# Graph-attention walks in steps of one tile of 128 edges instead of two, with eight tiles of each chunk scaled by ScalarE alone

## What is computed

```python
def gat_conv(x, W, a_src, a_dst, bias, src, dst, heads, out_ch, concat):
    h = (x @ W).reshape(n, heads, out_ch)
    al_s = jnp.einsum('nhc,hc->nh', h, a_src)
    al_d = jnp.einsum('nhc,hc->nh', h, a_dst)
    logits = jax.nn.leaky_relu(al_s[src] + al_d[dst], NEG_SLOPE)
    m = jax.ops.segment_max(logits, dst, num_segments=n)
    e = jnp.exp(logits - m[dst])
    denom = jax.ops.segment_sum(e, dst, num_segments=n)
    msg = h[src] * (e / denom[dst])[:, :, None]
    out = jax.ops.segment_sum(msg, dst, num_segments=n)
...
xn = _layernorm(x)
x = x + gnn(xn, edge_index, ...) + mix(xn, ...)
x = x + ffn(_layernorm(x), ...)
```

## Time and profile before

| what | us |
|---|---|
| median of 3 runs | 5648.19 (5645.58 to 5658.97) |
| the profiled execution, its own time | 5653.59 |
| its span from the first to the last instruction | 5651.8 |
| mean granted TensorE clock, as a share of full speed | 0.858 |
| POOL busy | 3660.6 |
| PE busy | 4335.7 |
| DVE busy | 3078.8 |
| ACT busy | 3010.0 |
| the walk of layer 1, first to last rescaling (L1268) | 223.7 to 2329.4 |
| the walk of layer 2, the same | 2565.1 to 4647.1 |

### The profile page before, as it was taken

How to read it: one execution, slowest core, us unless ns; L and a number is a source line. 1 busy time by engine, 2 the same in 40 slices (tenths; PEclk the granted TensorE clock), 3 DMA queues, 4 the chain that set the end, 5 groups by cost and what they waited for, 6 DMA issues and landing times. The chain is left out here.

```text
span 5651.8 us, 82730 instructions
## 1 busy us (share of the span) xinstructions
PE 4335.7 (77%) x21069; PEld 3336.5 (59%) x21069; DVE 3078.8 (54%) x8587; ACT 3010.0 (53%) x10079; POOL 3660.6 (65%) x3778
## 2 busy tenths in 40 slices
PE   7588888888888888775766667666565656899998
PEld 4466666666666666553444444444444435788887
DVE  5477777777777777654545545454454548211111
ACT  2677777777777777674545455453333334122221
POOL 0577777777777777457777777777777762344443
PEclk9789899999999998897778777787777775999999
DMA  5788878888888888435455444444556547443332
GB/s 188 236 242 242 243 234 244 241 243 241 243 243 244 240 243 238 144 119 145 138 143 143 138 144 138 143 140 140 170 159 171 159 119 238 143 129 129 127 127 74
DMA packets 427478, 1021.41 MB, mean 181 GB/s; under 512 B 115224, under 2 KB 207632, under 8 KB 426758
## 3 DMA queue, kind: packets, MB, share of 16 engines
q0 software_dynamic: 229312, 718.64, 44.4%
q1 hardware_dynamic: 197142, 296.44, 15.7%
q10 hardware_dynamic: 560, 1.05, 0.1%
HBM read 952.23 MB, written 65.48 MB: 180 GB/s over the span
## 5 line engine op out<-in xcount | busy, mean ns | idle before, releaser
L871 POOL DMA_INDIRECT walk_ring<-s_h,walk_index x3320 | 3200.0, 964 | 1169.5 <-issue 936.7
L1047 PE MATMUL walk_pM<-walk_ring,walk_hit 128*128 128x262 f32 (+1 forms) x9960 | 2776.8, 431 | 29.6 <-DVE acc L1275 18.0
L1047 PEld LDWEIGHTS walk_pM<-walk_ring,walk_hit 128*128 128x128 f32 x9960 | 2024.2, 211 | 449.9 <-issue 73.5
L906 ACT ACTIVATE walk_ring<-walk_ring 128x128 f32<-128x128 f32 (+1 forms) x6640 | 2134.3, 414 | 5.4
L1277 DVE TENSOR_TENSOR acc<-walk_pM,acc 128x520 f32 (+1 forms) x1494 | 834.3, 558 | 584.9 <-PE walk_pM L1047 564.4
L886 ACT ACTIVATE walk_ring<-walk_gap 128x40 f32<-128x40 f32 (+1 forms) x249 | 54.1, 259 | 1664.9 <-DVE walk_gap L1239 1664.9
L951 PE MATMUL walk_pC<-all_ident,walk_best 128*84 128x128 f32 (+1 forms) x166 | 61.7, 372 | 1032.2 <-DVE walk_best L1195 1032.2
L951 PEld LDWEIGHTS walk_pC<-all_ident,walk_best 128*84 128x84 f32 (+1 forms) x166 | 20.5, 124 | 1094.6 <-issue 1094.6
L1244 DVE TENSOR_TENSOR walk_hit<-walk_pK,walk_meta 128x512 f32<-128x512 f32 x830 | 561.1, 676 | 11.8
L2075 ACT ACTIVATE expert_hT<-expert_pH,expert_b 128x256 f32<-128x256 f32 x448 | 188.1, 471 | 594.7 <-PE expert_pH L2126 594.7
L1195 DVE TENSOR_TENSOR walk_best<-walk_ring,walk_dt 128x40 f32<-128x40 f32 (+1 forms) x249 | 47.1, 217 | 735.3 <-DMA walk_ring<-s_h,walk_index 735.2
(11 more groups left out here) (320 smaller groups left out, 4030.1 us busy)
## 6 DMA issues: line engine op xcount, KB each, us to landing
walk_hitT<-s_places SPq DMA_DIRECT2D x166, 640.0 KB, 5.5
expert_w<-in_fw_dram SPq DMA_DIRECT2D x56, 1024.0 KB, 5.4
walk_ring<-s_h,walk_index POOLq DMA_INDIRECT x3320
walk_xk<-s_xT SPq DMA_DIRECT2D x98, 128.0 KB, 4.3
down<-in_fw_dram SPq DMA_DIRECT2D x8, 1024.0 KB, 11.8
s_h<-first_h_out SPq DMA_DIRECT2D x7, 1056.0 KB, 4.3
finish_rows<-s_h SPq DMA_DIRECT2D x7, 1056.0 KB, 6.2
walk_resets<-s_resets SPq DMA_DIRECT2D x82, 84.0 KB
```

Of the source, the lines that this page charges most:

```text
L871: pool.indirect_dma_start(ring[:, r % RS, t, :], None, table, bass.IndirectOffsetOnAxis(ap=index[:, r % TS, t:t + 1], axis=0)).then_inc(ro ...
L906: last = nc.scalar.activation(row, row, ACT.Copy, scale=ring[:, r % RS, t, at + FH:at + FH + 1])
L1047: last = nc.tensor.matmul(pM[:, b, a, 0:WIDE], hit[:, (r * CGROUPS + g) % HBUF, t % GROUP, :], ring[:, r % RS, t, a * HALF_ROW:a * HALF_RO ...
```

## The change

TPS becomes 1: a step is one tile. There are now 1563 blocks and STEPS = 1563 + 48 = 1611. What was called a step in the loops of the engines is kept as a part of PART = 2 tiles, and a chunk still has CS = 10 parts and CT = 20 tiles; CHUNKS is ceil(1611 / 20) = 81. Each tile has its own PSUM buffer, its own window and its own add; a part of PE's work waits per tile for the add of three tiles before. Both engines read twenty window numbers a chunk, and ACT copies twenty goals. In layer 1 DVE scales the fourth head for the first three groups of four tiles alone (DVE_GROUPS = 3), and ACT scales all four heads of tiles 12 to 19. `gap` and `row_back` now share the memory of `pair`, to make room. The tables of the first pass are for 13 x 128 steps of one tile, not 7 x 128 of two.

```diff
-TPS = 2
+TPS = 1
...
-CT = CS * TPS
-CHUNKS = -(-STEPS // CS)
+PART = 2
+CT = CS * PART
+CHUNKS = -(-STEPS // CT)
...
+    DVE_GROUPS = 3
+    WROW = CT
...
-            return nc.values_load_multi_w_load_instructions(win[0:1, r % IS, 0:CS], engines=[engine], min_val=0, max_val=NW - 1,
+            return nc.values_load_multi_w_load_instructions(win[0:1, r % IS, 0:CT], engines=[engine], min_val=0, max_val=NW - 1,
...
-                        pool.wait_ge(multiplied, c * CS + s + 1)
+                        pool.wait_ge(multiplied, c * CT + (s + 1) * PART)
...
-                    for s in range(CS):
-                        last = nc.scalar.copy(goal[:, s, :, :], target[:, at[s], :, :])
+                    for t in range(CT):
+                        last = nc.scalar.copy(goal[:, t, :, :], target[:, at[t], :, :])
...
-                        for h in range(HA):
+                        for h in range(HA if t // GROUP < DVE_GROUPS else H):
...
-                    pe.wait_ge(added, c * CS + s + 1)
...
-                    for u in range(TPS):
-                        t = s * TPS + u
+                    for t in range(s * PART, (s + 1) * PART):
+                        pe.wait_ge(added, c * CT + t + 1)
                         for a in range(A):
-                            last = nc.tensor.matmul(pM[:, b, a, 0:WIDE], hit[...], ring[...], start=(u == 0), stop=(u == TPS - 1))
-                    last.then_inc(multiplied, 1)
+                            last = nc.tensor.matmul(pM[:, (r * CT + t) % PBUF, a, 0:WIDE], hit[...], ring[...], start=True, stop=True)
+                        last.then_inc(multiplied, 1)
...
                 def scale(c, i, r, g):
-                    if HA < H:
+                    if HA < H and g < DVE_GROUPS:
...
-                def add(c, i, r, s, w):
-                    b = (r * CS + s) % PBUF
-                    dve.wait_ge(multiplied, c * CS + s + 1 + AHEAD)
-                    dve.wait_ge(added, c * CS + s + PBUF)
+                def add(c, i, r, s, at):
+                    for t in range(s * PART, (s + 1) * PART):
+                        add_tile(c, i, r, t, at[t])
+
+                def add_tile(c, i, r, t, w):
+                    b = (r * CT + t) % PBUF
+                    dve.wait_ge(multiplied, c * CT + t + 1 + AHEAD)
+                    dve.wait_ge(added, c * CT + t + PBUF)
```

More of the change, by code:

```diff
@@ L533, in edge_work @@
                             pe.wait_ge(table_copied, q - 1)
-                        for u in range(TPS):
-                            last = nc.tensor.transpose(tables[q % 2][:, u * P:(u + 1) * P], (place, last_one, src)[n][:, j, u * P:(u + 1) * P],
+                        for u, j in enumerate(js):
+                            last = nc.tensor.transpose(tables[q % 2][:, u * P:(u + 1) * P], (place, last_one, src)[n][:, j, 0:P],
                                                        k["ident"][:, :])
@@ L599, in walk_pass @@
         row_ahead = m.sb("row_ahead", [1, RK + 1])
-        row_back = m.sb("row_back", [1, RK + 1])
         carry = m.sb("carry", [RK, 2])
-        pair = m.sb("pair", [P, 2, H, CT + 1])
-        gap = m.sb("gap", [P, H, CT + 1])
+        pairs = m.sb("pairs", [P, 2 * RK + 1])
+        pair = pairs[:, 0:2 * RK].rearrange("p (w h t) -> p w h t", w=2, h=H)
+        row_back = pairs[0:1, RK:2 * RK + 1]
+        gap = pair[:, 0, :, :]
         ratio = m.sb("ratio", [1, H])
@@ L941, in spread_targets @@
                     pe.sem_inc(part_seen, 1)
-                    for s in range(CS):
-                        for t in range(s * TPS, (s + 1) * TPS):
-                            last = nc.tensor.matmul(spread_t[:, t * SPREAD:(t + 1) * SPREAD], hitT[:, t * P:(t + 1) * P],
-                                                    goal[:, s, :, :].rearrange("p a q -> p (a q)"), start=True, stop=True)
+                    for t in range(CT):
+                        last = nc.tensor.matmul(spread_t[:, t * SPREAD:(t + 1) * SPREAD], hitT[:, t * P:(t + 1) * P],
+                                                goal[:, t, :, :].rearrange("p a q -> p (a q)"), start=True, stop=True)
                     last.then_inc(spread_out, 1)
@@ L1292, in chunk @@
                     scale(c, i, r, 3)
-                    add(c, i, r, 2, at[2])
+                    add(c, i, r, 2, at)
                     if mixing:
@@ L1297, in chunk @@
                         terms(*n)
-                    add(c, i, r, 3, at[3])
+                    add(c, i, r, 3, at)
                     if n:
@@ L1301, in chunk @@
                     hits(c, i, r, 4)
-                    add(c, i, r, 4, at[4])
+                    add(c, i, r, 4, at)
                     if n:
@@ L1305, in chunk @@
                     scale(c, i, r, 4)
-                    add(c, i, r, 5, at[5])
+                    add(c, i, r, 5, at)
                     if n:
@@ L1310, in chunk @@
                         mix_step(c, 5)
-                    add(c, i, r, 6, at[6])
+                    add(c, i, r, 6, at)
                     if n:
@@ L1315, in chunk @@
                         hits_turned(*later)
-                    add(c, i, r, 7, at[7])
+                    add(c, i, r, 7, at)
                     if mixing:
@@ L1322, in chunk @@
                         scale(*n, 0)
-                    add(c, i, r, 8, at[8])
-                    add(c, i, r, 9, at[9])
+                    add(c, i, r, 8, at)
+                    add(c, i, r, 9, at)
                     if mixing:
```

66 lines of the change are left out of this document (32 added, 34 removed).

## The result

The changed kernel takes 5721.7 us (median of 4 runs, 5718.56 to 5723.59), the kernel before, measured beside it, 5653.58 us: a ratio of 1.0116, 95% interval 1.0103 to 1.0128. It is slower, as forecast, and inside the range; but the forecast of 5930 us had the loss at over four times its size (its sum gave 281 us more than before, and 68 were measured). The profiled execution has a span of 5718.9 us against 5651.8, 67.1 us more.

What follows compares the result with a forecast made beforehand. DVE's own path was to replace POOL's gather issue as walk 1's bound, at 30.3 us a chunk: +323 us, with walk 2 at -42, together +281 on 5653.6; less 5.4 to the median, 5930 us, range 5680 to 6140.

Steps and rivals of the forecast that it cites:

- VectorE takes POOL's place in walk 1: Walk 1: DVE's own path of 29.2 us a chunk exceeds POOL's 25.7 and becomes the bound; chance 0.76.
- Ten additions at 0.91 us, less two scalings: DVE, walk 1: ten more adds a chunk cost +9.1 us, two scalings fewer -1.2 us, on a path of 20.1 us.
- Twenty windows, +1.2 us: DVE's register load, walk 1: twenty values take 3.17 us (lower end 1.92), adding 1.2 us of visible stall a chunk.
- Waits for PE, +1.1 us: DVE, walk 1: waits for PE's products take 1.1 us a chunk, between none and today's 2.92 us.
- Walk 2 at 25.5 us: Walk 2: POOL's pace stays the floor, 25.5 us a chunk (25.2 to 26.9), -42 us in all.
- The first pass, 0 +/- 5: Ahead of walk 1: more gathers and small compares while POOL is idle, counted as nothing, at most 5 us either way.
- POOL keeps the pace: Rival: DVE's waits and the saved scalings cover ten adds and the load, so it gets faster, 5546 us; chance 0.11.
- The wait for oneself is free: Rival: adds in walk 1 cost 0.60 us each, giving 27.2 us a chunk and 5678 us; chance 0.05.
- PE falls to its lower clock: Rival: short waits leave PE slow between the scans, walk 1 at 34.2 us a chunk, 6245 us; chance 0.08.

Runs made afterwards that it cites:

- e1: The changed kernel with VectorE scaling the fourth head in all five groups of a chunk instead of three: 5821.37 us, ratio 1.0291.
- e5: The changed kernel with VectorE's instructions reordered so some four additions a chunk stand behind another instead of eleven: 5588.79 us, ratio 0.9878.
- e2: The changed kernel with its slots of window numbers 88 bytes apart instead of 80: 5847.87 us, ratio 1.0341.
- e3: The kernel before with its slots of window numbers 48 bytes apart instead of 40, and `gap` in the memory of `pair`: 5660.38 us, ratio 1.0005.
- e8: The changed kernel with the first pass's table `through` turned on PE and stored in one transfer of 512-byte runs: 5705.0 us, ratio 1.0081.
- e9: The changed kernel with both the order of e5 and the turned table of e8: 5572.06 us, ratio 0.9847.
- e4: The kernel before, steps of two tiles, with only ScalarE scaling all four heads in a chunk's last eight tiles: 5664.32 us, ratio 1.0011.

## Why the prediction was right or wrong

**VectorE takes POOL's place in walk 1: right.** It waits for no rows, POOL waits, and two scalings move the chunk by 1.19 us (e1).

**Ten additions at 0.91 us, less two scalings: right.** 20.1 + 9.1 - 1.2 = 28.0 us was the path without the load's term. Measured it is 27.52 - 0.03 of waits for PE = 27.49 us, or 27.84 if the load's old stall of 0.35 us is put back: 0.16 us under the sum. e5 shows the 0.30 us between the pitches 5.9 times a chunk.

**Twenty windows, +1.2 us: the step that failed, with the next.** I chose 3.17 us for the load over 1.92. It took 1.35, and its stall disappeared: -0.35 instead of +1.2, which is 1.55 us a chunk, 1.55 x 81 = 126 us of the 225 us by which walk 1 was over-forecast (81 x 2.78). Two errors: between two rules for a slow load I took the costlier without a row for it, though both fitted every slow slot of before (the start decides, e2, e3); and I drew the price of a value from 1 and 10, 0.085 us, where the next ten cost 0.03 us each.

**Waits for PE, +1.1 us: the second term mis-sized.** They are 0.03 us a chunk, so 1.07 x 81 = 87 us too much. I let PE run behind VectorE at its old speed. But as VectorE no longer waits for rows, PE's 4.28 us of idle time in front of the transpose shrank to 0.86, and what had followed it, two tiles in 3.83 us at a clock of 0.50, takes 2.00 us. I used this row for a rival in which PE gets slower and never for its own forecast in the other direction. Whether it was PE's clock that took these waits away, or that VectorE itself is later (its path grew by 7.4 us), no run separates; the clock's part is my reading. The remaining 0.16 us of 2.78 (13 us) is that of the path, not traced further.

**Walk 2 at 25.5 us: right**, 25.37 (within 10 us over 81 chunks). Its waits for rows took most of the additions; they fell from 6.0 us a chunk to 255.5 / 80 = 3.2:

```profile
DVE walk_best L1196 <- DMA walk_ring<-s_h,walk_index: 255.5, 79, 11.0
```

**The first pass, 0 +/- 5: wrong by 12 us**, in the other direction. I counted gathers and compares and passed over the through stores, whose runs halved to 4 bytes and nearly doubled in number, 896 to 1664 a transfer. e8 shows them. Some 4.7 us were there before those stores, within my 5. The end and the gap between the walks added another 12 us that I had at nothing. The timelines show half of it: from walk 2's last rescaling row to the end of its last addition it is 13.9 us (4705.8 to 4719.7) where it was 8.0 (4647.1 to 4655.1), with the last additions one by one 0.64 us apart. The other half was not traced.

**The rivals.** POOL keeps the pace: not what happened, though e5 and e9 show that with another order its pace is within reach, at 25.7 and 25.8 us. The wait for oneself is free (5678 us): the nearest in time, and by the wrong mechanism: the 0.91 us are there in every chunk, and e5 gains 133 us by avoiding six of them a chunk. That a semaphore after each of a row of copies costs nothing extra, as the Trainium skill, "VectorE: DVE Perf Modes", section on the DRAIN you can't avoid, has it, does not hold for these additions, each of which waits for the one right before it: 0.91 us against 0.61. PE falls to its lower clock: the opposite, 1.00 for 0.91, as its one long wait shrank. The Trainium skill, "TensorE: Matmul & The Clock Gate", section on psum-queue depth-cycling, tells of a kernel whose clock went up and down with short idle times between groups of matmuls; the new short waits here did not do that.

## What to carry to other kernels

Price a stall where the engine that has it is the bound: the same kind of load stall cost nothing in the kernel before (e3) and 3.1 us apiece in e2, and the same shift of scalings nothing in e4 and 95 us in e1. When an engine becomes the bound, its partners' idle times shrink too; if one of them had lost clock behind a long idle time, forecast that it gets it back. Do not take low GB/s for the bound before a wait for a transfer shows it. Put other work of the same engine between two instructions that depend on each other, and look at the length of a store's contiguous runs whenever a tile size is halved.

## What the runs showed of the hardware

A load of registers from on-chip memory is slow when its source starts 8 bytes past a multiple of 16, counted from the table's start: 2.3 instead of 1.07 us for ten values, 4.5 instead of 1.35 us for twenty. An addition of 128x520 that depends on the one before starts 0.91 us after it, one with other work between takes 0.61 us of the engine. PE's granted clock was 1.00 over the changed kernel's walk 1, with some eight waits a chunk, nearly all of 1.4 us or less, and 0.50 right behind a wait of 4.28 us in the kernel before. In e2, whose slow loads make PE wait up to 4.2 us in every second chunk, it was 0.97 (300 to 2200 us). Two stores of 1664 runs of 4 bytes, some 13 KB in all, made ScalarE wait up to 17.5 us for the large stores behind them when SyncE issued them and 15.7 us when GpSimd did; as one store of 26 runs of 512 bytes, 2.8 us.
